# A CIN tower on one core: fused multiply-adds on VectorE, one more chunk in three fp32r passes, a smaller fold on GpSimd

## The reference

```
e = stack([tbl_f[ids[:, f]] for f in range(32)], axis=1)      # [512, 32 fields, 32 d]
prev = e
for W in (filter_0, filter_1):                                 # each to 128 maps
    z = einsum('bhd,bmd->bhmd', e, prev).reshape(b, h * m, d)
    prev = relu(einsum('bpd,pn->bnd', z, W[0]))
    outs.append(prev)
h = concat([sum(concat(outs, 1), -1), dense_ctx], 1)
y = relu(relu(h @ W_top1 + b_top1) @ W_top2 + b_top2) @ W_top3
```

## Time and profile before

| | |
|---|---|
| median of 3 runs | 843.94 us (843.12 to 845.85) |
| span of the profiled execution | 841.7 us |
| PE busy | 834.0 us (99%) |
| DVE busy | 803.9 us (96%) |
| ACT busy | 782.8 us (93%) |
| POOL busy | 726.7 us (86%) |

### The profile page before, as it was taken

The page is one execution under the profiler, slowest core; times in us unless marked ns, Lnnn a source line. Parts: engine busy times, 40 slices in busy tenths (PEclk is TensorE's granted clock), DMA queues, the critical chain, the costliest instruction groups (busy, mean ns, idle before and its releaser), DMA issues.

```text
span 841.7 us, 17220 instructions
## 1 busy us (share of the span) xinstructions
PE 834.0 (99%) x3595; PEld 670.1 (80%) x3595; DVE 803.9 (96%) x877; ACT 782.8 (93%) x2779; POOL 726.7 (86%) x550
## 2 busy tenths in 40 slices
PE   8999999999999999999999999999999999999998
PEld 6688888888888888888888888888888888888777
DVE  7699999999999999999999999999999999999996
ACT  4799999999999999999999999999999999999984
POOL 5899888999888899888899888899988799988871
PEclk9999999999999999999999999999999999999999
DMA  5541132332132232122232122332123223212000
GB/s 154 181 134 50 46 85 79 82 85 62 32 84 78 83 84 72 33 73 78 83 84 81 34 62 80 82 83 84 44 50 84 78 84 84 51 44 76 1 13 1
DMA packets 62101, 60.17 MB, mean 71 GB/s; under 512 B 26203, under 2 KB 37083, under 8 KB 62078
## 3 DMA queue, kind: packets, MB, share of 16 engines
q1 hardware_dynamic: 57982, 57.80, 23.3%
q0 software_dynamic: 4096, 2.11, 2.9%
HBM read 55.51 MB, written 4.31 MB: 71 GB/s over the span
## 4 chain that ended last, share of the span: by engine, by line
PE 94%; DVE 2%; DMA 1%; POOL 1%; issue 1%; SPq 0%; ACT 0%; DVEq 0%
PE ps_y L895 27%; PE ps_y L903 27%; PE ps_y L896 27%; PE ps_c L868 3%; PE ps_c L878 3%; PE ps_c L877 2%; PE ps_c L876 2%; POOL gat L447 1%; DVE csum L737 1%; PE ps_c L874 1%; DVE prod L724 1%; DMA prod<-w 0%; DMA gat<-table,rows 0%; DMA ids_and_bounds_sb<-ids_and_bounds 0%; PE ps_y L999 0%
## 5 line engine op out<-in xcount | busy, mean ns | idle before, releaser
L559 ACT ACTIVATE prod<-ps_y,es 128x128 f32<-128x128 f32 x2560 | 719.7, 490 | 37.3 <-PE ps_y L903 34.0
L737 DVE TENSOR_REDUCE csum<-prod 128x64 f32<-128x1664 f32 (+2 forms) x256 | 478.6, 1870 | 0.2
L895 PE MATMUL ps_y<-w_hi,c_both 128*128 128x512 f32 x1024 | 415.4, 406 | 1.8 <-POOL w_lo L454 1.0
L903 PE MATMUL ps_y<-w_hi,c_both 128*128 128x512 f32 x1024 | 399.6, 390 | 0.0
L896 PE MATMUL ps_y<-w_lo,c_both 128*128 128x512 f32 x1024 | 399.5, 390 | 0.0
L724 DVE TENSOR_TENSOR prod<-ps_y,es 128x512 f32<-128x512 f32 x384 | 256.0, 680 | 23.6 <-PE ps_y L903 22.4
L436 POOL TENSOR_TENSOR prod<-prod 128x768 f32<-128x768 f32 (+1 forms) x128 | 240.3, 1878 | 35.9 <-ACT prod L559 28.7
L895 PEld LDWEIGHTS ps_y<-w_hi,c_both 128*128 128x128 f32 x1024 | 192.4, 188 | 54.2 <-issue 10.4
L896 PEld LDWEIGHTS ps_y<-w_lo,c_both 128*128 128x128 f32 x1024 | 192.4, 188 | 48.2 <-issue 8.2
L903 PEld LDWEIGHTS ps_y<-w_hi,c_both 128*128 128x128 f32 x1024 | 192.2, 188 | 42.1
L426 POOL TENSOR_TENSOR z<-first,second 128x512 f32<-128x512 f32 x155 | 198.2, 1295 | 25.0 <-PE ps_c L874 24.9
(11 more groups left out here) (119 smaller groups left out, 290.1 us busy)
## 6 DMA issues: line engine op xcount, KB each, us to landing
second<-et_scratch SPq DMA_DIRECT2D x155, 256.0 KB, 3.8
first<-et_scratch SPq DMA_DIRECT2D x31, 256.0 KB, 3.3
et_scratch<-gat SPq DMA_DIRECT2D x62, 64.0 KB
prod<-w SPq DMA_DIRECT2D x4, 512.0 KB, 4.5
h_scratch<-h_sums SPq DMA_DIRECT2D x120, 2.0 KB
gat<-table,rows_now POOLq DMA_INDIRECT x116, 2.4
wt_sb<-wt SPq DMA_DIRECT2D x2, 512.0 KB
rows_now<-rows SPq DMA_DIRECT2D x30, 2.0 KB, 1.8
```

What stands on the lines that cost most here:

```text
L559: last = nc.scalar.activation(prod[:, buffer_of(g, u), h // 2, :, h % 2], ps_y[:, bank_of(g, u, k), j * N:(j + 1) * N], ACT.Copy, scale=es ...
L737: nc.vector.tensor_reduce(csum[:, g.r, maps, u], prod[:, buffer_of(g, u), fields_folded(g, u) // 2:F // 2, maps, :].rearrange("p a n t -> ...
L895: nc.tensor.matmul(out, hi, w_hi, start=True, stop=False)
L903: nc.tensor.matmul(out, lo, w_hi, start=False, stop=True).then_inc(y_ready, 1)
```

## The change

DVE no longer writes products of its own. For each of its three banks it takes a partner among ACT's banks (2 to 0, 4 to 1, 7 to 5), waits until ACT has scaled it, and adds its own products to the partner's fields with four `scalar_tensor_tensor` of 128 elements in place of one `tensor_tensor` of 512. `prod` therefore holds 20 fields in place of 32; GpSimd folds 4 of them (6 in the last group) and DVE's reductions run over 16 (14). A fold waits for the DVE banks whose sums it reads. DVE no longer waits for its own reductions, since ACT's banks already did. Layer 0's chunk 0 is split and multiplied in three fp32r passes like chunks 1 to 3, behind bank 0 of tile 1 in place of bank 6 of tile 0; ACT rounds it behind bank 1 of tile 0, GpSimd splits it in tile 0. The raw filters get memory of their own instead of lying in `prod`, and a wait of ACT in group 0 goes.

```diff
-WHOLE = 1
+WHOLE = 0
 ACT_BANKS = ((0, 1, 3, 5, 6),) * TG
-DVE_BANKS = tuple(tuple(k for k in range(NK) if k not in a) for a in ACT_BANKS)
-FOLD = 6
-FOLD_LAST = (10, 10, 10, 8)
+PARTNER = {2: 0, 4: 1, 7: 5}
+DVE_BANKS = (tuple(PARTNER),) * TG
+SCALED = HB * len(ACT_BANKS[0])
+FOLD = 4
+FOLD_LAST = (6, 6, 6, 6)
...
-        prod = sb("prod", [P, BUFS, F // 2, N, 2])
+        prod = sb("prod", [P, BUFS, SCALED // 2, N, 2])
+        w1_raw = sb("w1_raw", [P, F, N])
+        w0_raw = sb("w0_raw", [P, 2 * KP, N])
...
+        def place_of(u, k):
+            return HB * ACT_BANKS[u].index(k)
...
             def fold(g, u):
                 count = fields_folded(g, u)
-                last_bank = (2 * count - 1) // HB
-                pool.wait_ge(act_scaled, signals(ACT_BANKS, g, u, last_bank))
-                pool.wait_ge(dve_scaled, signals(DVE_BANKS, g, u, last_bank))
+                folded_banks = ACT_BANKS[u][:(2 * count - 1) // HB + 1]
+                pool.wait_ge(act_scaled, signals(ACT_BANKS, g, u, folded_banks[-1]))
+                pool.wait_ge(dve_scaled, signals(DVE_BANKS, g, u, max(k for k in DVE_BANKS[u] if PARTNER[k] in folded_banks)))
...
-            Z_LO_AT = {1: (1, 2), 2: (3, 4)}
+            Z_LO_AT = {0: (0,), 1: (1, 2), 2: (3, 4)}
...
-                        if number == 0 and (u, k) == (2, 0):
-                            act.wait_ge(w1_lo_ready, NK - 2)
-                            act.wait_ge(w1_last_lo, 2)
...
-            Z_HI_AT = {(1, 1): (0, 3), (1, 2): (0, 5), (1, 3): (1, 0), (1, 4): (1, 5)}
+            Z_HI_AT = {(1, 0): (0, 1), (1, 1): (0, 3), (1, 2): (0, 5), (1, 3): (1, 0), (1, 4): (1, 5)}
...
-                    wait(dve, reduced, g.times(TG * HALVES, (u + 1 - BUFS) * HALVES))
                 dve.wait_ge(y_ready, g.times(TG * NK, u * NK + k + 1))
-                fields = slice(HB * k, HB * (k + 1))
-                pairs = slice(HB // 2 * k, HB // 2 * (k + 1))
-                nc.vector.tensor_tensor(
-                    prod[:, buffer_of(g, u), pairs, :, :],
-                    ps_y[:, bank_of(g, u, k), :].rearrange("p (a n t) -> p a n t", n=N, t=2),
-                    es[:, g.r, u, fields].rearrange("p (a t) -> p a t", t=2).unsqueeze(2).to_broadcast([P, HB // 2, N, 2]),
-                    ALU.mult).then_inc(dve_scaled, 1)
+                dve.wait_ge(act_scaled, signals(ACT_BANKS, g, u, PARTNER[k]))
+                for j in range(HB):
+                    h, place = HB * k + j, place_of(u, PARTNER[k]) + j
+                    summed = prod[:, buffer_of(g, u), place // 2, :, place % 2]
+                    last = nc.vector.scalar_tensor_tensor(out=summed, in0=ps_y[:, bank_of(g, u, k), j * N:(j + 1) * N],
+                                                          scalar=es[:, g.r, u, h:h + 1], in1=summed,
+                                                          op0=ALU.mult, op1=ALU.add)
+                last.then_inc(dve_scaled, 1)
...
-            Z_USED_AT = ((0, 6), (1, 6), (2, 1), (2, 4), (2, 6))
+            Z_USED_AT = ((1, 0), (1, 6), (2, 1), (2, 4), (2, 6))
```

More of the change, by code:

```diff
@@ L174, in tower @@
         y_sb = sb("y_sb", [1, B])
-        w1_raw, w0_raw = (prod[:, b, :, :, :].rearrange("p a n t -> p (a n t)").rearrange("p (h n) -> p h n", n=N)
-                          for b in (2, 1))
         ids_sb = ids_and_bounds_sb[:, 0:TILES]
@@ L557, in scale @@
                 for j in range(HB):
-                    h = HB * k + j
-                    last = nc.scalar.activation(prod[:, buffer_of(g, u), h // 2, :, h % 2],
+                    h, place = HB * k + j, place_of(u, k) + j
+                    last = nc.scalar.activation(prod[:, buffer_of(g, u), place // 2, :, place % 2],
                                                 ps_y[:, bank_of(g, u, k), j * N:(j + 1) * N], ACT.Copy,
@@ L736, in reduce @@
                 maps = slice(half * N // HALVES, (half + 1) * N // HALVES)
-                nc.vector.tensor_reduce(csum[:, g.r, maps, u], prod[:, buffer_of(g, u), fields_folded(g, u) // 2:F // 2, maps, :].rearrange("p a n t -> p n a t"),
+                nc.vector.tensor_reduce(csum[:, g.r, maps, u], prod[:, buffer_of(g, u), fields_folded(g, u) // 2:SCALED // 2, maps, :].rearrange("p a n t -> p n a t"),
                                         AX.XY, ALU.add).then_inc(reduced, 1)
@@ L1052, in filters_by_bank @@
 def filters_by_bank(w1):
[L1054 to L1061, removed]
+    return np.ascontiguousarray(w1.reshape(F, N, N).transpose(1, 0, 2))
 def row_picks():
```

## The result

| | before | after |
|---|---|---|
| median, us (4 runs each) | 844.05 | 874.89 |
| lowest to highest, us | 843.12 to 845.85 | 873.66 to 876.04 |
| profiled execution, us; its span | 843.94; 841.7 | 875.77; 874.0 |

The ratio is 1.0366, with a 95% interval of 1.0352 to 1.0380: slower by 30.8 us. The forecast was 18.9 us slower.

What follows compares the result with a forecast made beforehand. PE's list was taken to bound each group. 30 groups at 0.78 of wait less 0.17 saved, plus 1.5, less 0.9, gave +18.9 us on 843.94: 862.8 us; own range 855 to 869, wider range 849 to 885.

Steps and rivals of the forecast that it cites:

- the chain of GpSimd: GpSimd's split of chunk 1, queued behind chunk 0's split and ACT's new rounding, makes PE wait: 0.78 us per group.
- GpSimd's wait for the rounding: Before the split of chunk 0, GpSimd idles about 0.8 us, released by ACT's new rounding.
- 0.70 + 0.08: PE at chunk 1: 0.70 us of waiting for GpSimd's split and 0.08 of restart per group.
- 0.17: PE, chunk 0 of layer 0: three fp32r passes of 0.69 us replace 0.86, saving 0.17 us per group.
- ACT ... 0.52 us ... Hidden: ACT gains chunk 0's rounding, 0.52 us; its load of 24.6 us per group stays under PE's 24.9, so no cost.
- the pitch of DVE's fused operation: DVE's 48 short fused instructions per group: 0.20 us each, load 21.7 us; DVE takes over at 0.283.
- the row of 0.27: DVE, 128 elements with per-partition scalar in SBUF: 0.35 us less 0.08 of overlap, giving 0.27 and a load of 25.1.
- The group with the top layers' piece: Group 30, where GpSimd's 2.41 us piece follows a later fold: 1.5 us more of PE's wait, bounds 0 and 2.4.
- The -0.9 in the last group: PE's 0.79 us wait for DVE in the last group, plus the restart, counted as gone: -0.9 us.
- PE alone: Rival, 11%: GpSimd's chunk 1 split is in time, so only PE's shorter list counts: 837.9 us.
- DVE as the bound: Rival, 9%: DVE's short instructions cost over 0.283 us each; 888 us at 0.30, 962 at 0.35.
- Half of it: Rival, 5%: GpSimd's chain about 0.6 us shorter than counted, so PE's saving and wait cancel: 844 us.

Runs made afterwards that it cites:

- e10: e6 with a constant 1.0 in place of the per-partition scalar in DVE's fused operation, leaving out a multiplication: 838.28 us, one run.
- e1: The kernel after without the split of chunk 0, which is one fp32 matmul again: 845.45 us, ratio to before 1.0015.
- e2: The kernel before with only chunk 0's split, rounding and three passes placed as in the kernel after: 886.55 us, ratio to before 1.0507.
- e3: The kernel after with PE taking chunks 1 and 2 later: 862.57 us, ratio to before 1.0221.
- e5: The kernel after with chunk 0 rounded by GpSimd instead of ACT: 865.90 us, ratio to before 1.0257.
- e7: The kernel before with two idle activations a group added on ACT: 844.21 us, ratio to before 1.0001.
- e4: The kernel after with a constant 1.0 in place of the per-partition scalar in DVE's fused operation: 870.22 us, one run.
- e6: The kernel after with chunk 0 rounded by GpSimd and PE taking the later chunks later: 862.54 us, ratio to before 1.0219.
- e8: e6 with the roundings of chunks 2 and 3 later among ACT's products: 846.01 us, ratio to before 1.0027.

## Why the prediction was right on the side and short by 12 us

**Right: the chain of GpSimd.** ACT waits, GpSimd waits, PE waits, at the places named. GpSimd's wait for the rounding was put at 0.8 and is 0.53. PE's was put at 0.70 + 0.08 and is 0.41 + 0.10. Two small things stand beside it: PE saves not 0.17 but 25.08 - 24.84 = 0.24 a group (e10), and it waits a little for a bank of ACT's that the rounding delayed, 0.36 from 423.02 to 423.38 instead of 0.23, and 0.10 of restart. 0.51 + 0.23 - 0.24 = 0.50, measured 0.54, forecast 0.61; the group is 25.62, forecast 25.7. e1, e2 and e3 each move this term as a chain of steps must.

**Missing: the start of the loop.** The step "ACT ... 0.52 us ... Hidden" failed. It counted ACT's load and its slack, and not what a few more instructions do to a loop: 8 x 1.59 = 12.7 us, as large as the whole miss of 12.1. It is in no rival either. The measured 874.9 lies above the forecast's own 855 to 869, and within 849 to 885 only because that range was widened for DVE's pitch, which cost nothing here: that the range holds is luck. The trace of before shows no price for the missing term: its loop's branch, at 447.30 us, lies within an unbroken run of products, and no packet of instructions comes between 136 and 750 us. e5 and e7 together show the cause, and e7 that it costs only where the work behind it is awaited. The Trainium skill, "Runtime: NRT & Kernel Launch", section on instruction fetch mechanics, says that an engine holds a limited stretch of its list and that a taken branch to a target outside it waits for a fetch. The traces agree that such a fetch is waited for: 366 records in ACT's loop leave the queue at 14 to 18 packets, 374 and 375 bring 54 to 58, five a round, with the pause.

**Mis-sized: the pitch of DVE's fused operation**, 0.20 taken, 0.258 measured. The value was that of the form without a scalar for each partition, and e4 has 0.198 for that; the row of 0.27 showed the form with it. The estimate of 0.26 from the Trainium skill ("VectorE: DVE Perf Modes", the section on the TRN2 errata) came to the right total by another way: it put more on the fixed part of reading PSUM, and e4 shows the fixed part as the rows of before have it and 0.06 us for the scalar. It did no harm to the sum, since at 24.55 us a group DVE stays under the 25.7 forecast. It leaves DVE little time to make up for late work of ACT: with the pitch of 0.198 in e10, e6's loss is gone; for e3 that is argued from DVE's 25.15 busy of 25.71 us.

**Ends.** The group with the top layers' piece was put at 1.5 us; it is 27.45 us, 1.8 over a normal one. The -0.9 in the last group came to -0.24 for the whole last stretch. Groups 0 and 1 are 2.45 us longer; I have not assigned that. Group 0 takes 18.4 to 21.0 us in the runs here, also in kernels that differ only in tables for later groups.

**Rivals.** PE alone: 24.84 us a group is real, but only in e10, which leaves work out. DVE as the bound: not in the kernel after (e4), but 24.5 of 25.1 us in e8, the next limit at once. Half of it: the wait was shorter than counted by about 0.3 us, not 0.6, so it did not cancel the saving.

## What to carry to other kernels

Moving work to an engine with slack is priced by its place, not by its load: ask what stands behind each new wait in that engine's order, and put the work where the engine that reads it can be late. Count the instructions of a loop's body on each engine, not only their time: ACT's, a few instructions longer, began every round with a pause, and what stands first behind the branch must then not be what another engine is waiting for. When an engine is at 98% of the group, as DVE was, it can hardly make up for a wait that it catches elsewhere, so a faster first engine needs the second one relieved as well.

## What the runs showed of the hardware

- ACT's loop of 366 records runs without a packet in the instruction queue (none from 136 to 750 us in the kernel before), the ones of 374 and 375 with five packets of about 8 KB a round (0.47 MB over 57) and a pause of 1.0 to 1.6 us behind the branch (after, e2, e3, e7). PE's longer loop and DVE's of 308 records bring none (e5: 18 packets in all).
- On DVE a scalar_tensor_tensor of 128 elements with PSUM and SBUF sources has a pitch of 0.198 us with a constant and 0.258 with a scalar for each partition.
- The bracketed wait of a matmul is smaller than what it costs: 0.24 shown, 0.41 by the starts, and 0.10 more until the next matmul.
